# ScalarE issues the store of each unit's sums itself, in all six attention stages

## The reference

```python
scores = einsum('bqhd,bkhd->bhqk', q, k) / sqrt(8)      # self: 256 keys (layer 2: windows of 64); cross: 1601 keys
top_s, top_i = top_k(scores, 16)                        # cross attention of layer 2 only
attn = softmax(scores)                                  # of layer 2's cross attention: softmax(top_s)
out = einsum('bhqk,bkhd->bqhd', attn, v)                # then an output projection and the residual
```

## Time and profile before

| what | us |
|---|---|
| median of 3 runs | 4722.28 (4713.96 to 4735.18) |
| the profiled execution | 4714.82 |
| its span in the trace | 4713.1 |
| PE, DVE, ACT, POOL busy | 3444.2, 3582.4, 2859.7, 612.9 |

### The profile page before, as it was taken

The page is one execution under the profiler, slowest core; times in us unless marked ns, Lnnn a source line. Parts: engine busy times, 40 slices in busy tenths (PEclk is TensorE's granted clock), DMA queues, the critical chain, the costliest instruction groups (busy, mean ns, idle before and its releaser), DMA issues. The chain is left out here.

```text
span 4713.1 us, 74839 instructions
## 1 busy us (share of the span) xinstructions
PE 3444.2 (73%) x28020; PEld 1497.4 (32%) x28020; DVE 3582.4 (76%) x5514; ACT 2859.7 (61%) x5351; POOL 612.9 (13%) x1338
## 2 busy tenths in 40 slices
PE   2669999976789999848466666666566656579987
PEld 2223333332323333323132223223232222235543
DVE  6658889826578888436799999999999999732223
ACT  1456888843547878627377777777776776621223
POOL 1122122001324232003011010101000000000000
PEclk7798999986879999968577767777777777789999
DMA  4553343205533342045211010101111110000000
GB/s 135 146 132 93 85 112 86 51 22 160 122 88 96 88 102 67 17 119 124 70 40 40 22 39 22 39 22 39 27 34 32 25 21 11 3 29 28 21 0 9
DMA packets 277494, 285.16 MB, mean 61 GB/s; under 512 B 38800, under 2 KB 246040, under 8 KB 276248
## 3 DMA queue, kind: packets, MB, share of 16 engines
q1 hardware_dynamic: 277144, 280.53, 23.6%
HBM read 152.08 MB, written 127.18 MB: 59 GB/s over the span
## 5 line engine op out<-in xcount | busy, mean ns | idle before, releaser
L1312 ACT ACTIVATE prob<-xa_ps 128x512 f32<-128x512 f32 (+1 forms) x2880 | 1563.4, 597 | 409.5 <-PE xa_ps L1207 385.8
L1399 DVE TENSOR_REDUCE mpart<-ring 128x1 f32<-128x400 f32 (+2 forms) x2816 | 1294.4, 526 | 285.6 <-PE ring L1155 282.3
L1155 PE MATMUL ring<-k_st,q_st 52*128 52x400 bf16 (+2 forms) x3584 | 863.9, 371 | 364.0 <-ACT s_sb L1294 315.4
L1226 PE MATMUL xa_ps<-prob,va 128*16 128x256 f32 (+1 forms) x9984 | 852.0, 424 | 0.5 <-ACT prob L1312 0.5
L1207 PE MATMUL xa_ps<-q_st,k_st 55*128 55x256 bf16 x5504 | 623.0, 300 | 58.2 <-ACT prob L1312 44.1
L1202 PE MATMUL xa_ps<-neg_id,un 128*128 128x128 bf16 (+1 forms) x3328 | 365.0, 276 | 361.7 <-ACT prob L1312 359.9
L1285 ACT ACTIVATE un<-s_sb 128x1601 fp8e4<-128x1601 f32 x256 | 392.8, 1536 | 344.4 <-DVE s_sb L1425 344.4
L1155 PEld LDWEIGHTS ring<-k_st,q_st 52*128 52x128 bf16 x3584 | 254.5, 100 | 888.2 <-ACT s_sb L1294 394.0
L1294 ACT ACTIVATE s_sb<-ring 128x400 f32<-128x400 f32 (+1 forms) x1024 | 471.9, 524 | 31.8 <-PE ring L1155 23.4
L1425 DVE MATCH_REPLACE8 s_sb<-m8b,s_sb 128x1601 f32<-128x1601 f32 x256 | 478.8, 1946 | 0.0
L1418 DVE MATCH_REPLACE8 s_sb<-mpart,s_sb 128x1601 f32<-128x1601 f32 x256 | 478.7, 1945 | 0.0
(11 more groups left out here) (227 smaller groups left out, 3370.5 us busy)
## 6 DMA issues: line engine op xcount, KB each, us to landing
k_st<-kc_dram SPq DMA_DIRECT2D x192, 300.2 KB, 5.4
o_dram<-o_sb SPq DMA_DIRECT2D x192, 128.0 KB, 1.9
kc_dram<-k SPq DMA_DIRECT2D x72, 300.0 KB, 3.4
q_st<-q_dram SPq DMA_DIRECT2D x80, 192.0 KB, 4.0
kc_dram<-k SPq DMA_DIRECT2D x72, 200.0 KB, 3.8
ctx_t<-in_ctxT SPq DMA_DIRECT2D x16, 800.5 KB, 4.8
k_st<-k_dram SPq DMA_DIRECT2D x48, 192.0 KB, 5.0
kc_dram<-k SPq DMA_DIRECT2D x24, 300.8 KB, 3.3
```

Source lines behind the costliest of these rows:

```text
L1155: nc.tensor.matmul(ring_ps[:, r % BANKS, 0:w], q_st[rows, b % NQ, 2 * t + pl, qt * P:(qt + 1) * P], k_st[rows, slot_of(n), pl, c0:c0 + w], ...
L1226: last = nc.tensor.matmul(av_ps[32 * k:32 * k + VW, n % 2, :], va[0:sizes[j], b % NVB, j, G * t + k, :], prob[0:sizes[j], s % NPROB, (2 * ...
L1312: nc.scalar.activation(prob[0:size, s % NPROB, hf * 512:(hf + 1) * 512], x_ps[0:size, (2 * s + hf) % XBANKS, :], ACT.Exp, scale=HEAD_SCALE ...
L1399: nc.vector.tensor_reduce(mpart[:, n % 4, row, c:c + 1], ring_ps[:, r % BANKS, 0:chunks[c][1]], AX.X, ALU.max).then_inc(g["red"].sem, 1)
```

## The change

The store leaves SP's program and goes into ACT's: behind the copy of a unit's sums ACT waits for that copy to be written (`ocopy`), at the first unit of a batch from the third batch on also for the load that last read this half of `o_dram` (`nl`), and issues the store itself. Nothing else is changed; the transfer and its semaphore `ost` are the same.

```diff
     ocopy_at = by_step((unit_end[n], n) for n in range(NU))
-    ostore_at = by_step((unit_end[n] + 2, n) for n in range(NU))
...
-            def store_o(n):
-                b, t = divmod(n, NG)
-                sp.wait_ge(g["ocopy"].sem, g["ocopy"].at(n + 1))
-                sp.dma_start(p.o_dram[b % 2, t], o_sb[:, t]).then_inc(g[f"ost{t}"].sem, 16)
-
...
-                for n in ostore_at.get(k, []):
-                    store_o(n)
...
                 if n >= NG:
                     act.wait_ge(g[f"ost{n % NG}"].sem, g[f"ost{n % NG}"].at(16 * (n // NG)))
                 nc.scalar.activation(o_sb[:, n % NG, :], av_ps[:, n % 2, :], ACT.Copy).then_inc(g["ocopy"].sem, 1)
+                act.wait_ge(g["ocopy"].sem, g["ocopy"].at(n + 1))
+                if n % NG == 0 and n >= 2 * NG:
+                    act.wait_ge(g[f"nl{n // NG % 2}"].sem, g[f"nl{n // NG % 2}"].at(32 * (n // NG // 2)))
+                nc.scalar.dma_start(p.o_dram[n // NG % 2, n % NG], o_sb[:, n % NG]).then_inc(g[f"ost{n % NG}"].sem, 16)
```

## The result

The changed kernel took 4800.7 us in the median of 4 runs (4789.09 to 4808.73), the kernel before 4728.73 us in runs beside them: ratio 1.0155, 95% interval 1.012 to 1.019. The profiled execution took 4789.09 us, span 4787.2 us, 74.3 us more than the profiled one of before. The forecast was 4784 us, range 4742 to 4838.

What follows compares the result with a forecast made beforehand. Bounds: PE in layers 0 and 1's cross stages, ACT briefly at unit ends; DVE in layer 2's; a PE-ACT loop in self stages. 34 + 30 + 1 less 3 gave 62 us, 4777, plus 7.5: 4784 us; range 4742 to 4838.

Steps and rivals of the forecast that it cites:

- The delay of a cross unit: ACT at a cross unit's end: copy, release, issue and step make the next instruction 0.54 us later.
- What of it reaches the end in the cross stages: Cross stages of layers 0 and 1: PE already waits there and is elsewhere full, so 34 us reach the end.
- The self stages: Three self stages: 0.53 us a unit on the loop, 51 us, less 21 absorbed by waits, 30 us.
- the loop has no slack on either engine: Self units: PE and ACT form a closed loop of 3.19 us, so ACT's 0.53 us a unit counts on it.
- the waits would absorb 7 us a stage: Self stages: irregular waits for rows of maxima and POOL's parts shrink, absorbing 7 us each, 21 in all.
- the prediction's own signs of being wrong: ACT's issue time unlike SP's, PE's added wait below ACT's delay, ACT waiting for `nl`, or SP limiting self stages.
- Layer 2's cross stage: DVE takes scores 5.4 us after they are ready, so the delay drowns; only the last unit feels it, 1 us.
- The wait for `nl`: At the first unit of a batch, the load is done 1.2 us before ACT asks; cost zero.
- The issue is cheap: Rival, 12%: on ACT only the wait for its own copy costs, SP's relief offsets most; 4725 us.
- Issues collide: Rival, 20%: ACT's issue waits for one of SP's, or itself takes 0.73 us; 4812 to 4840 us.
- PE catches up: Rival, 7%: cross stages regain half the lost time, self loop has hidden slack; +31 us, 4753 us.
- Faster: Rival, 3%: SP holds the self stages back, PE's waits for maxima vanish, ACT's part is hidden; 4703 us.

Runs made afterwards that it cites:

- the second: Profile of the changed kernel run once more, nothing altered; 4794.09 us, ratio 1.0149 to the kernel before.
- `e_cross01`: Against the kernel before, ACT issues the store only in the cross stages of layers 0 and 1, SP elsewhere; 4774.43 us, ratio 1.0109.
- `e_two`: Against the changed kernel, ACT issues each store as two transfers of 64 partitions; 4988.58 us, ratio 1.0566 to the kernel before.
- `e_self`: Against the kernel before, ACT issues the store only in the three self stages, SP elsewhere; 4737.15 us, ratio 1.0029.
- `e_cross2`: Against the kernel before, ACT issues the store only in layer 2's cross stage, SP elsewhere; 4720.92 us, ratio 0.9991.
- `e_late1`: Against the kernel before, ACT waits and issues the store at the end of the step after the copy; 4717.67 us, ratio 0.9986.
- `e_late2`: Against the kernel before, ACT waits and issues the store at the end of the second step after the copy; 4725.65 us, ratio 1.0008.
- `e_pool`: Against the kernel before, GpSimd issues the stores in place of SP, at the same steps; 4726.33 us, ratio 1.0006.
- `c_shift_now`: Against the changed kernel, copy, ACT's wait and issue moved one exponential later; 4747.48 us, ratio 1.0059 to the kernel before.
- `e_wait_only`: Against the kernel before, ACT waits for its own copy in all stages, SP still issues the store; 4737.98 us, ratio 1.0023.
- `c_shift`: Against the kernel before, only the copy of sums moved one exponential later, SP still storing; 4716.79 us, ratio 0.9993.

## Why the prediction was right, and where its sum was not

The forecast was right in sign, in place and nearly in size: 4784 for 4800.7 us. Of the 17 us between them 6 are the base, since the runs of the kernel before that were shown had a median of 4722.3 and those beside the result one of 4728.7. The change itself was forecast at 62 us and measured 72. That the sum came so near is in part luck: the self stages were over-priced by 16 us, and a term of about the same size, PE's clock, was missing. With the self stages at their 14 us the same sum would have been 46.

**The delay of a cross unit** (0.54 us forecast) measured 0.85 - 0.27 = 0.58 us. Its terms in the profile after are the copy of 0.39, a release of 0.03, an issue of 0.33 and a step behind it of 0.10 us (726.60 to 726.70), less 0.27. Only the step was off, forecast at 0.05 from SP. SP's 338 ns for ACT's unseen issue was near ACT's 326. In a self unit SP's 418 ns was too much, ACT took the same 326 ns, and the delay was 0.85 - 0.35 = 0.50 us for 0.53.

**What of it reaches the end in the cross stages** (34 us) was right for what it described. PE's wait at a unit's end went to 1.2 us in layer 0 as forecast, to 1.0 us in layer 1, and idle time grew by 16.8 + 15.1 = 31.9 us, with 17 for each stage expected. Nothing gave it back. The one unit in six without a visible wait pays too: its wait stands at `kf` (3.0 to 6.4 us).

**The missing term is PE's clock.** The forecast held the busy time of PE fixed. It isn't: 7.0 + 5.9 us in the first profile, 17.3 + 12.3 in the second, 22.5 + 5.8 in `e_cross01`, for the same matmuls. The granted clock says so in the same rows, 1.00 and 0.99 before, 0.95 to 0.99 after. So the cross part costs some 50 us (49 by the medians of `e_cross01`) and not 34, and the amount varies between executions far more than idle time does. That the longer pauses bring the lower clock is supported by the dose. In layer 0's cross stage 16 to 17 us of added idle go with a clock of 0.95 to 0.99 and 42 us in `e_two` with 0.91; the runs whose idle time is as before (`e_self`, `e_cross2`, `e_late1`, `e_late2`, `e_pool`, `c_shift_now`) stand at 1.00. `e_wait_only` has 0.99 with 3.4 us more idle, `c_shift` 0.99 with less idle than before, so 0.01 means nothing. It is a correlation over the runs; none held the clock.

**The self stages** were over-priced: 51 us on the loop less 21 absorbed, 30 in all, against 14 us measured by `e_self` and 9.5 us of added idle in the changed kernel. The step that failed is "the loop has no slack on either engine". The unit of the earlier trace rows took 3.19 us from copy to copy and takes 246.15 - 242.95 = 3.20 us in the profile after. The step that comes most often in layer 0's stage went from 2.99 us (9 of 31) to 3.20 us (10 of 31), 0.21 and not 0.53. The slack was in the rows: ACT waited 0.17 to 0.36 us for PE before its copies, and the pause has eaten it (no such wait stands ahead of the copy at 246.15; in the whole stretch these waits went from 24 to 12). Further, the exponential starts 0.17 us behind the start of `mT`, where it was 0.32 us. These stages are measured less sharply than the cross stages: first to last copy of the three is 354.6 us before and 367.4 after, but 345.4 and 347.3 us in `e_cross2` and `e_cross01`, whose self stages are those of before.

The other half of the step, that the waits would absorb 7 us a stage, was too large: the wait for rows of maxima shrank by 2.9 us in layer 0 and from 5.1 to 3.8 us in layer 2, the one for POOL's parts by 0.2 in layer 1. Of this, 2.9 us is not much more than what executions differ by without the change (4.6 us in `e_cross01`, 6.9 in `e_cross2`). Nor did `e_pool` and `e_late1`, which relieve SP as well, gain time clear of noise. So two of the prediction's own signs of being wrong came in the self stages: ACT's issue took another time than SP's, and PE's added wait is less than ACT's delay.

**Layer 2's cross stage** (1 us) held in the time: `e_cross2` is no slower than before within its interval (upper end +0.03%), and DVE is busy 1675.13 us for 1675.17. But the 4.1 us in the rows are more than chance. Nearly all of them arise in the last unit, behind DVE's last MAX8. From its start to the last copy it is 46.0 to 47.7 us in all six profiles in which ACT stores there with the copy in its old place (`e_cross2` among them), and 43.3 to 43.7 us in the five in which it doesn't. PE's idle time in that piece is 10.4 to 11.6 us in the six and 10.6 to 10.9 in the five. Its busy time is 34 to 37 us for 33, at a granted clock of 0.76 to 0.81 for 0.84 to 0.85. With the copy moved it is the other way round (`c_shift` 47.3 us, `c_shift_now` 43.5). So this is PE's clock again, in a stretch of which the forecast had only said that the last unit can feel the delay; what decides it stays open, and no run's time shows it.

**The wait for `nl`** (0) held but for one case in two profiles, 0.2 us in layer 2's self stage. The row of one batch, on which the zero stood, doesn't speak for all 36.

**The rivals.** *The issue is cheap*: no; the wait alone costs 0.23%, the whole 1.55%. But its idea holds in a place the rival didn't name: behind queued work the issue is free (`e_late1`, 0.9986). *Issues collide*: the time, 4812 us, came near by luck, the mechanism isn't there: 192 issues on ACT of 326 to 360 ns beside a busy SP, and SP's own small transfers take 704 ns in the median in layer 0's self stretch, 712 before. In the Trainium skill, the page "Perfetto Trace Analysis", section "DMA Instruction — HWDGE (DVE, Sync)", has a lock on a shared generator within an issue's time; in the changed kernel no wait for it shows on ACT. The 44 issues on ACT that overlap one of SP take 327 ns in the median, the other 148 take 326. The issues of up to 1839 ns in `e_two` stay unexplained, but they don't go with SP's issues either. *PE catches up*: not in the cross stages; in the self stages it is what happened, by hidden slack. *Faster*: ACT's delay was five times the 0.12 us from which it would have decided. (The time of *PE catches up*, +31 us, is 3 us too high by the prediction's own sum of 62.)

In sum: 32 us idle in cross stages and some 13 to 30 of clock, 10 to 14 us in self stages, nothing in layer 2's cross stage; that is 55 to 76 us, with 72 measured (4800.7 - 4728.7).

## What to carry to other kernels

Before moving a DMA issue to the engine that made the data, look at what that engine has in execution when it comes to the issue: right behind its own result it pays the rest of that instruction, the release and the whole issue in series, here 0.58 us a unit; one step later in the program the same issue hides beneath work already queued and costs nothing, even where it leaves at the same moment, 0.03 us behind the copy. When a stall lands on a PE that is nearly full, price the granted clock beside the idle time; here it added 40 to 95% to the idle time that layer 0's and 1's cross stages gained together. Where an engine of a loop still waits for another, as ACT did for 0.17 to 0.36 us ahead of its copies, the loop has slack, and a delay elsewhere in it had to fill that first.

## What the runs showed of the hardware

- An issue of a DMA on ACT (326 ns) ran beside an exponential that ACT had taken before (711.29 to 711.62 within 711.13 to 711.75, in `e_late1`), and the exponentials around it had no gap. Busy times of an engine and of its issues can overlap.
- An issue for 64 partitions took 452 to 1839 ns, median 488, one for 128 partitions 326 to 360 (to 393 in `e_late1`), on the same engine with the same row length. Open why. GpSimd took 542 to 725 ns for the whole one.
- The same 6021 matmuls took 523 us busy at a granted clock of 1.00, 530 at 0.99, 541 at 0.96, 546 at 0.95 and 569 at 0.91 (layer 0's cross stage), some 0.8 to 1.3% for each hundredth of clock.
- MAX8 in layer 2's cross stage is recorded with a median of 1953 ns in the profile of before and of 1824 ns after, while first and last start lie equally far apart, 1792.5 and 1792.6 us:

```profile
L1414 DVE MAX8 mpart<-s_sb x256: 1809/1953/2061, 2287.9 to 4080.4; 128x8 f32<-128x1601 f32 x128
```

```profile
L1410 DVE MAX8 mpart<-s_sb x256: 1773/1824/1869, 2353.4 to 4146.0; 128x8 f32<-128x1601 f32 x128
```

The step from a MAX8's start to DVE's next start is 1728 ns in the median in both, less than the recorded length in either. So the recorded length of this instruction is no measure of the time that it holds the engine.
